# A six-layer network on one core: where the layers' semaphores are cleared, and which engine casts h in the first four blocks of an expert layer

## The reference, cut to what matters

```python
x = x + scan_layer(groupnorm(x))                # selective scan in four directions
x = x + neighbourhood_attention(groupnorm(x))   # 12 heads, 7 x 7 window
t = t + quantised_block(layernorm(t))           # integer softmax attention and MLP
t = t + moe_gated(layernorm(t))                 # 16 experts of 512, top 2, plus a shared expert of 1024
t = t + attention(layernorm(t))                 # plain softmax attention, one head over each image
t = t + moe_gelu(layernorm(t))                  # 8 experts of 768, top 2, with biases
```

## Time and profile before

| | |
|---|---|
| median of 3 executions | 1158.23 us (1155.89 to 1160.6) |
| profiled execution, its own time | 1158.88 us |
| its span, first to last instruction | 1157.0 us |
| busy share of PE, DVE, ACT, POOL | 75%, 72%, 51%, 28% |
| mean granted TensorE clock | 0.818 |
| scan layer ends at | 251.5 us |
| neighbourhood layer ends at | 389.0 us |
| quantised layer ends at | 648.5 us |
| gated expert layer (m) ends at | 914.0 us |
| attention layer ends at | 976.7 us |
| second expert layer (g) ends at | 1153.5 us |

### The profile page before, as it was taken

The page is one execution under the profiler, slowest core; times in us unless marked ns, Lnnn a source line. Parts: engine busy times, 40 slices in busy tenths (PEclk is TensorE's granted clock), DMA queues, the critical chain, the costliest instruction groups (busy, mean ns, idle before and its releaser), DMA issues. The chain is left out here.

```text
span 1157.0 us, 16408 instructions
## 1 busy us (share of the span) xinstructions
PE 872.7 (75%) x5650; PEld 588.5 (51%) x5650; DVE 833.8 (72%) x1651; ACT 586.4 (51%) x912; POOL 326.3 (28%) x304
## 2 busy tenths in 40 slices
PE   7699999967989565677645286999999295469980
PEld 3333333343588412223343175989988154359980
DVE  6689999965665589999857755888885514558862
ACT  2755454312433276899914223767762132168960
POOL 0036666632000021222100043222224300434435
PEclk8899999987999755555566688999999599579995
DMA  8096665412000000000000363999970201649922
GB/s 272 10 238 153 178 170 150 109 30 53 1 1 2 18 1 1 1 1 1 1 1 1 94 189 86 249 262 272 266 193 29 68 1 36 195 136 267 269 80 82
DMA packets 65938, 120.45 MB, mean 104 GB/s; under 512 B 11264, under 2 KB 40896, under 8 KB 65856
## 3 DMA queue, kind: packets, MB, share of 16 engines
q1 hardware_dynamic: 62784, 113.12, 36.5%
q0 software_dynamic: 3072, 6.30, 1.8%
HBM read 101.89 MB, written 17.50 MB: 103 GB/s over the span
## 5 line engine op out<-in xcount | busy, mean ns | idle before, releaser
L456 POOL TENSOR_TENSOR hC<-hs,Cb 128x1024 f32<-128x1024 f32 x47 | 110.8, 2357 | 124.4 <-DVE hs L495 124.4
L1819 POOL CAST m_h_hi<-m_h 128x512 f16<-128x512 f32 x62 | 53.9, 869 | 240.0 <-DVE m_h L1894 239.9
L495 DVE TENSOR_TENSOR_SCAN hs<-ps_l,dBu 128x1024 f32<-128x1024 f32 x48 | 109.9, 2290 | 2.8 <-ACT ps_l L587 1.2
L655 PE MATMUL ps_l<-hC,selT 128*96 128x512 f32 x192 | 93.2, 609 | 1.5 <-POOL hC L456 1.5
L640 PE MATMUL ps_l<-du,sel 96*128 96x512 f32 x192 | 90.5, 593 | 1.4 <-DVE dBu L488 1.4
L587 ACT ACTIVATE ps_l<-d_sp,Am 128x1020 f32<-128x1020 f32 x48 | 53.5, 1115 | 71.5 <-DVE hs L495 71.3
L1902 DVE TENSOR_TENSOR m_h_lo<-m_h,m_h_hi 128x512 f16<-128x512 f32 x62 | 42.8, 692 | 46.5 <-POOL m_h_hi L1819 41.9
L2092 ACT ACTIVATE m_act<-ps_m 128x512 f32<-128x512 f32 x62 | 36.8, 593 | 64.8 <-PE ps_m L2167 60.6
L2185 PE MATMUL ps_m<-m_wd_hi,m_h_hi 128*128 128x192 f16 x248 | 63.0, 254 | 8.4 <-DVE m_h_lo L1902 4.9
L1515 PE MATMUL ps_l<-q_xi,identh 128*128 128x512 f16 x48 | 28.5, 594 | 49.0 <-DVE q_ex L1270 28.2
L1143 POOL TENSOR_SCALAR q_e<-q_qi 128x512 int16<-128x512 f16 x48 | 29.8, 622 | 119.3 <-ACT q_qi L1410 60.6
(11 more groups left out here) (501 smaller groups left out, 2689.1 us busy)
## 6 DMA issues: line engine op xcount, KB each, us to landing
d_sp<-scan_d SPq DMA_DIRECT2D x48, 512.0 KB, 4.5
m_sta<-in_m_ua SPq DMA_DIRECT2D x25, 512.0 KB, 4.9
m_stb<-in_m_ub SPq DMA_DIRECT2D x50, 256.0 KB, 6.3
m_std<-in_m_dn SPq DMA_DIRECT2D x25, 384.0 KB, 7.8
g_std<-in_g_dn SPq DMA_DIRECT2D x15, 576.0 KB, 6.2
g_sta<-in_g_ua SPq DMA_DIRECT2D x15, 384.0 KB, 3.7
g_stb<-in_g_ub SPq DMA_DIRECT2D x30, 192.0 KB, 4.5
scratch_x<-zero SPq DMA_DIRECT2D x1, 4416.0 KB, 19.3
```

The lines of the kernel that those rows point to most:

```text
L456: pool.tensor_tensor(hC[:, n % 2, :], hs[:, n % 2, :], Cb[:, which(n), :], ALU.mult).then_inc(weighted, 1)
L495: v.tensor_tensor_scan(hs[:, n % 2, ::step], dA(n)[:, ::step], dBu[:, n % 2, ::step], 0.0, ALU.mult, ALU.add).then_inc(scanned, 1)
L655: mm = pe.matmul(ps[0:DI, 6 + half, :], selT[:, n % NG, :], hC[:, n % 2, half * BANK:(half + 1) * BANK], start=(n == STEPS), stop=(m == ST ...
L1819: pool.tensor_copy(h_hi[:, b % 2, q, :], src).then_inc(h_high, 1)
```

## The change

`ctx.clear()` goes. A layer's semaphores stay allocated in a second stack (`hold`) after the layer's end; the next layer's SP clears them inside its own block, after that layer's first loads, and they are released when that layer ends. The attention layer takes part in this (its semaphores are cleared in the last layer). The last layer's semaphores are released and not cleared. In the gated expert layer the cast to `h_hi` of the first EARLY = 8 steps (the four shared blocks) is done by ACT after silu, with a semaphore of its own, and POOL starts with its 16 scatters. For layer g EARLY is 0.

```diff
@@ class Ctx
-        self.nc, self.stack, self.sems = nc, stack, []
+        self.nc, self.stack, self.sems, self.hold = nc, stack, [], ExitStack()
     def sem(self, name):
-        self.sems.append(self.stack.enter_context(self.nc.semaphore(name)))
+        self.sems.append(self.hold.enter_context(self.nc.semaphore(name)))
         return self.sems[-1]
-    def clear(self):
-
-        with self.nc.Block() as block:
-            @block.sync
-            def _(sync):
-                for s in self.sems:
-                    sync.sem_clear(s)
+    def end(self, K):
+        if "last" in K:
+            K["last"].hold.close()
+        K["last"] = self
+
+
+def clear_last(sync, K):
+    for s in K["last"].sems:
+        sync.sem_clear(s)
@@ scan_layer (const is K), neighbour_layer, quantised_layer, expert_layer, at the end; attention_layer gains it
-        ctx.clear()
+        ctx.end(K)
@@ neighbour_layer, quantised_layer, attention_layer: SP, after its constant loads
+                clear_last(sync, K)
@@ expert_layer
     FIRST = len(plan)
+    EARLY = FIRST * PAIRS
...
+        early_high = S("early_high")
@@ expert_layer, POOL
-                for k in range(STEPS * PAIRS):
-
-                    while moved < 2 * NT and (not gated or (k >= 2 and moved < 4 + 3 * (k - 2))):
+                for k in range(EARLY, STEPS * PAIRS):
+
+                    while moved < 2 * NT:
                         scatter(moved)
                         moved += 1
@@ expert_layer, DVE, low(k)
-                    v.wait_ge(h_high, k + 1)
+                    if k < EARLY:
+                        v.wait_ge(early_high, k + 1)
+                    else:
+                        v.wait_ge(h_high, k + 1 - EARLY)
@@ expert_layer, ACT, after silu of step k (and split_down where it stands)
+                        if k < EARLY:
+                            act.wait_ge(h_full, k + 1)
+                            if b >= 2 and q == 0:
+                                act.wait_ge(down, b - 1)
+                            act.activation(h_hi[:, b % 2, q, :], h32[:, k % 3, :], ACT.Copy).then_inc(early_high, 1)
@@ program, after the last layer
+        K["last"].hold.close()
+        ctx.hold.close()
```

More of the change, by code:

```diff
@@ L685, in _ @@
                         mm.then_inc(res_ps, 1)
-        ctx.clear()
+        ctx.end(const)
 NH = 12
```

## The result

The changed kernel takes 1139.1 us (median of four executions, 1135.4 to 1141.1) against 1157.3 us for the kernel before on the same chip, a ratio of 0.9825 with a 95% interval of 0.980 to 0.985. The medians themselves are 18.2 us apart (a ratio of 0.9843), which lies within that interval. Beside other kernels on another chip the ratio came out at 0.9827 (0.980 to 0.9855). The forecast was 1139.3 us, in a range of 1134 to 1145. The profiled execution has a span of 1136.8 us and an own time of 1138.9.

A forecast was written before the change was run, and what follows sets the result against it. It took SP's lone clears at five layer ends and POOL's scatter list in layer m to be on the path; 16.2 + 2.7 = 18.9 us off gave 1139.3 us against the median, range 1134 to 1145.

The forecast's parts named there:

- The pauses: Five layer ends where only SP works, clearing semaphores: removing clears (14.7 us) and barriers (1.5 us) saves 16.2 us.
- a layer that starts behind a barrier costs nothing: Starts of the next layers without a pause: taken as 0, with bounds of 0 and 12.8 us.
- The clears' new places: Clears on SP behind each next layer's first loads: cost 0; in layer m 14 us of cover remain.
- POOL's list: Layer m's 16 scatters without casts between them: last one ends 2.7 us earlier, bounds 0 and 4.7 us.
- The walk: Layer m's new order reckoned: five scatter starts fall under DVE instructions, holds adding 2.0 us.
- rival B: Layer m: nothing holds the scatters, so 4.7 us go there; 1137.3 us in all, chance 0.25.
- A: The forecast itself: pauses gone, layer m's scatters held about as before; 1139.3 us, chance 0.50.
- eight casts of 0.63 us: Layer m's casts on ACT: 5.0 us in all, 8 us of cover, one long wait for gate at k = 2.
- C: Layer m's first routed block comes no earlier, so only the pauses count; 1142.0 us, chance 0.17.
- D: Neighbourhood layer: TensorE's clock keeps its low level, up to 75 us more; 1214 us, chance 0.03.
- E: Layer starts: engines need the pause, so the inner 12.8 us return as idle; 1152.1 us, chance 0.05.
- the clock +-2 us in layer m: TensorE's clock rise after its wait for rows in layer m may shift: +-2 us, taken as 0.

The follow-up runs named there:

- e1: Changed kernel with only the clears moved; the casts of layer m stay on POOL between scatters as before: 1141.1 us, 0.9823 of the kernel before.
- e7: Changed kernel plus one clear block at the very end for the last layer's 57 semaphores: 1143.2 us, 0.9857 of the kernel before.
- f4: Changed kernel with layer m's clears done ten times over, 480 clears behind the loads: 1139.2 us, 0.9821 of the kernel before.
- e2: Kernel before with only the casts moved to ACT in layer m, clear blocks kept: 1156.7 us, 0.9961 of the kernel before.
- e4: Changed kernel with down_block(2) of layer m put ahead of the first routed rows' transposes: 1135.7 us, 0.9779 of the kernel before.
- e5: Changed kernel with down_block(2) and down_block(3) of layer m put ahead of the transposes: 1140.4 us, 0.9822 of the kernel before.
- e3: Changed kernel with the clears ahead of each layer's first loads instead of behind them: 1149.9 us, 0.9909 of the kernel before.
- e6: Changed kernel with DVE's low of layer m's first eight steps cut to 8 of 512 columns: 1140.0 us, 0.9836 of the kernel before.
- e8: Changed kernel with all casts of layer m back on POOL, behind the 16 scatters: 1147.4 us, 0.9894 of the kernel before.
- f1: The changed kernel run again, unchanged, on another chip: 1139.6 us, 0.9827 of the kernel before.

## Why the prediction was right

**The pauses**: 16.2 us reckoned, 16.2 in the trace, and e1 and e7 each confirm a part. (The 16.2 of the layer table are the forecast's own rows. What the trace after adds is that nothing stands in their place.) The count of clears times 57 ns, with 0.3 us for the barrier, was all it took, and the attention layer's start as the control was the right row for "a layer that starts behind a barrier costs nothing".

**The clears' new places**: 0, right, though the argument for layer m was too careful. I gave SP 14 us of cover; f4 used 28.5 us of clears without harm, since what follows isn't needed at once.

**POOL's list**: 2.7 us reckoned and 2.7 measured (25.5 to 22.8). The walk found five holds of 2.0 us in sum (0.43, 0.26, 0.24, 0.06, 1.03); the trace has four of 2.0 (0.43, 0.51, 0.06, 1.00). Three of the four have the size of the walk's. That the sum is equal is partly luck, and in e2, e4 and e5 it was 0.9 us. Layer m gained 0.8 us more than this, 0.7 of it because its first scatter started 26.4 instead of 27.1 us after the barrier. In the other profiles, but for e3, that start lies between 26.0 and 26.8; I take it for the clock, but no run isolates it.

**What holds a scatter**: the rule of the Trainium skill (SBUF - State Buffer, "Who interferes with whom"), by which a `tensor_tensor` would not stall descriptor generation, doesn't hold for these indirect DMAs, by e6 and e8; the rival B with it, whose 1137.3 us lie within what the medians can't tell from A anyway.

**ACT**: eight casts of 0.63 us, the last ending at 685.5 us, where 688 was forecast, and the one long wait for gate (4.9 us, before the third cast) where it was expected. C needed the chain to be late, and it was done 8.8 us before its next duty. D and E did not come.

**What the sum left out** is that layers move which the change leaves alone: -3.8 (quantised), +1.3 (attention), +1.3 (scan) and +0.6 us (neighbourhood) here. The first two are the clock, as shown above. The other two are not: the granted clock over the scan layer is 0.95 in both profiles, and over the neighbourhood layer it is higher after (0.94) than before (0.91). What they are stays open. The forecast gave the clock +-2 us in layer m and a rival of its own in the neighbourhood layer (D), but no term in the quantised and the attention layer, where it moves up to 4 us between executions. That the total came out within 1 us of the forecast is partly luck, for these four differences nearly cancel (-0.6), and the medians of the kernel before alone lie between 1157.3 and 1160.6 us on the four chips.

## What to carry to other kernels

Housekeeping that one engine does alone between two barriers costs its whole length on all engines; inside the next stage, behind that stage's first loads, ten times as much was free, and ahead of them most of it was paid where the stage's first work waited for a load. To see that, compare points inside a layer, not only its length, which the clock can shift by as much the other way. When a queue is the chain, look for what else lies in it (here casts between indirect DMAs), but moving that work behind the chain is not enough: it needs an engine that is free at the time. And work put into a wait of TensorE is worth less than its length: down_block(2), 3.0 us long in f1, made the stretch behind it 1.4 us shorter at equal clock when it was moved, and a later rise of the clock took 1.6 us back.

## What was not expected of the hardware

- A GpSimd indirect DMA that starts under a VectorE `tensor_tensor` or `scalar_tensor_tensor` with both inputs in SBUF ends 0.84 to 0.86 us after that instruction, 1.0 to 2.0 us long instead of 0.97. The first scatter of a series is longer in any case (1.68 us in layer m), and a gate, with one input in PSUM, holds none.
- On the chip of the first group, in three of four profiles (e2, e4, e5), TensorE's instructions came with unexplained pauses of 0.2 to 1.1 us for some 10 us, from within the series of 16 indirect DMAs to 2 us past its end; in e1 and in the ten profiles of other runs no such series is seen. e1 has casts between the scatters. In e2 they use up the wait for the rows, so that the transposes start no later than elsewhere (52.4 us into the layer), and cost nothing; in e4 and e5 the transposes come at 56.0 and 59.2 us. What causes them stays open.
- The same layer is up to 4 us shorter or longer from one execution to the next by where the granted clock rises (0.58 or 0.97 over the same 35 matmuls).
- The low level that follows TensorE's 10 us wait in layer m lasts between 2.7 and 5.9 us beyond the first transposes in profiles in which this part of the kernel is the same (f1 and e7), which takes 7.95 or 9.55 us to the second.
